# A four-layer graph network on one core: a leading dimension of 2 or 4 on the DRAM side of the loops' loads and stores

## The reference

```python
# layer 0: an MLP per edge, summed by destination
h = relu(concat(x[dst], x[src], edge_attr_32) @ W1 + b1)
out = segment_sum(h @ W2 + b2, dst)
# layer 1: degree-normalised sum over edges, by destination
agg = segment_sum(x[src] * ci[src][:, None], dst) * cj[:, None]
out = relu(where(in_deg > 0, agg, x) @ W.T + b)
# layer 2: symmetric normalisation, summed by source
agg = segment_sum(norm[:, None] * x[dst], src)
out = relu(agg @ W.T + b)
# layer 3: gates from the 40 edge features, a cutoff of the distance, summed by source
gate = silu(edge_attr_40 @ W1.T + b1) @ W2.T + b2 + adapt_logit
agg = segment_sum(gate * h[dst] * (cw * node_mult[dst])[:, None], src)
x = layernorm(x + layer(x))        # after each of the four
```

## Time and profile before

| | us |
|---|---|
| median of 3 runs | 24622.62 |
| lowest and highest | 24618.94, 24633.03 |
| span of the profiled execution, first to last instruction | 24578.9 |
| PE busy | 11303.0 (46%) |
| POOL busy | 11058.2 (45%) |
| DVE busy | 9805.1 (40%) |
| ACT busy | 3908.0 (16%) |
| DMA, queue row of SP (q1) | 9.9% of 16 engines |
| DMA, queue row of ScalarE (q10) | 4.6% of 16 engines |

### The profile page before, as it was taken

The page is one execution under the profiler, slowest core; times in us unless marked ns, Lnnn a source line. Parts: engine busy times, 40 slices in busy tenths (PEclk is TensorE's granted clock), DMA queues, the critical chain, the costliest instruction groups (busy, mean ns, idle before and its releaser), DMA issues. The chain is left out here.

```text
span 24578.9 us, 300511 instructions
## 1 busy us (share of the span) xinstructions
PE 11303.0 (46%) x63600; PEld 9551.4 (39%) x63601; DVE 9805.1 (40%) x26342; ACT 3908.0 (16%) x10412; POOL 11058.2 (45%) x11410
## 2 busy tenths in 40 slices
PE   5555555555544545555664333433532233333334
PEld 5555545454433333333443333333421133333334
DVE  3444444444555555551113444444411133333335
ACT  1000000000111111113331001100111122222221
POOL 3444444444433444435554444444344444444443
PEclk9999999999756566665555555555555555555555
DMA  4222222222111111113332111112222222121221
GB/s 97 66 64 66 65 66 65 65 65 65 43 31 32 34 34 35 34 32 92 89 89 60 54 53 55 54 54 55 58 64 57 58 57 56 54 56 56 55 57 47
DMA packets 1574947, 1407.00 MB, mean 57 GB/s; under 512 B 982793, under 2 KB 1441692, under 8 KB 1570447
## 3 DMA queue, kind: packets, MB, share of 16 engines
q1 hardware_dynamic: 597320, 636.63, 9.9%
q0 software_dynamic: 410000, 462.80, 7.9%
q10 hardware_dynamic: 567508, 306.27, 4.6%
HBM read 984.46 MB, written 420.15 MB: 57 GB/s over the span
## 5 line engine op out<-in xcount | busy, mean ns | idle before, releaser
L1743 POOL DMA_INDIRECT order<-l_msg,l_uring x6250 | 6046.0, 967 | 6894.5 <-ACT l_uring L2012 4152.7
L1886 PE MATMUL ps<-l_ordb,l_ohs 128*128 128x49 f32 x15040 | 3319.1, 413 | 4897.1 <-DVE acc L1786 3125.6
L1886 PEld LDWEIGHTS ps<-l_ordb,l_ohs 128*128 128x128 f32 x15040 | 3248.2, 331 | 4967.9 <-DVE acc L1786 3170.3
L545 POOL DMA_INDIRECT l_rows<-btab,l_sd x3125 | 2978.5, 953 | 3292.3 <-DMA l_sd<-in_sd 2081.4
L1786 DVE TENSOR_TENSOR acc<-acc,ps 128x49 f32 x7520 | 1526.5, 206 | 3901.5 <-DMA btab<-pro_stb 2159.2
L1082 POOL DMA_INDIRECT l_rows<-y,l_sd x1875 | 1828.2, 975 | 2733.2 <-DMA l_sd<-in_sd 2199.7
L701 PE MATMUL ps<-l_ohe,l_hid 128*128 128x32 f32 x6250 | 1372.3, 365 | 2538.9 <-issue 2537.6
L701 PEld LDWEIGHTS ps<-l_ohe,l_hid 128*128 128x128 f32 x6250 | 1436.5, 323 | 2492.0 <-issue 2491.7
L686 PE MATMUL ps<-l_rhs,l_lhs 64*128 x6250 | 1421.9, 423 | 280.2 <-issue 119.3
L1303 PE MATMUL ps<-l_okey,l_hlo 128*128 128x294 bf16 x2520 | 716.4, 405 | 1784.5 <-issue 647.7
L686 PEld LDWEIGHTS ps<-l_rhs,l_lhs 64*128 64x128 f32 x6250 | 1350.8, 328 | 341.7 <-issue 341.7
(11 more groups left out here) (313 smaller groups left out, 14418.7 us busy)
## 6 DMA issues: line engine op xcount, KB each, us to landing
l_ordb<-order SPq DMA_DIRECT2D x752, 250.0 KB
l_dstb<-ids SPq DMA_DIRECT2D x250, 600.0 KB
order<-l_msg,l_uring POOLq DMA_INDIRECT x6250
order<-l_zero ACTq DMA_DIRECT2D x125, 775.0 KB
l_eat<-in_ea40P SPq DMA_DIRECT2D x625, 120.0 KB
gates<-l_made ACTq DMA_DIRECT2D x625, 120.0 KB
l_gin<-gates SPq DMA_DIRECT2D x125, 600.0 KB
l_rows<-btab,l_sd POOLq DMA_INDIRECT x3125
```

The lines of the kernel that those rows point to most:

```text
L545: pool.indirect_dma_start(rows[:, t, :], None, d["btab"], bass.IndirectOffsetOnAxis(ap=sd[:, t, 0:1], axis=0)).then_inc(gat[c], 16)
L1743: pool.indirect_dma_start(d["order"], bass.IndirectOffsetOnAxis(ap=uring[:, t:t + 1], axis=0), msg[:, t, :], None).then_inc(sc[c], 16)
L1886: done = t.matmul(red[b % 2][:, k * MW:(k + 1) * MW], ohs[b][:, k, :], ordb[b][:, k, 0:MW], start=True, stop=True)
```

## The change

A helper `queues` gives the DRAM side of a transfer a leading dimension of 2 (`FEW`) or 4 (`SOME`): rows `(a p)` become `a` times `p`. It is put around 16 transfers that SP and ScalarE issue in the loops of the four layers; the SBUF side stays one dimension of partitions. Nothing else changes: same bytes, same buffers, same waits, same order.

```diff
--- before.py
+++ after.py
...
@@ -98,6 +98,16 @@
 
 def bc(ap, shape):
     return ap.to_broadcast(shape)
+
+
+FEW, SOME = 2, 4
+
+
+def queues(ap, k):
+
+    if len(ap.shape) == 2:
+        return ap.rearrange("(a p) f -> a p f", a=k)
+    return ap.rearrange("(a p) t f -> a p t f", a=k)
 
 
 def gnn(nc, a, out):
...
@@ -504,12 +514,12 @@
-                sp.dma_start(dstb[:, ds((g % 2) * GE, GE)], d["ids16"][0:1, ds(g * GE, GE)].to_broadcast([WN, GE])).then_inc(dstb_in, 16)
+                sp.dma_start(dstb[:, ds((g % 2) * GE, GE)], queues(d["ids16"][0:1, ds(g * GE, GE)].to_broadcast([WN, GE]), SOME)).then_inc(dstb_in, 16)
-                    sp.dma_start(sd[:, chunk_cols(c), :], a["sd"][:, ds(t0, CT), :]).then_inc(sd_in[c], 16)
+                    sp.dma_start(sd[:, chunk_cols(c), :].rearrange("p t k -> p (t k)"), queues(a["sd"][:, ds(t0, CT), :].rearrange("p t k -> p (t k)"), FEW)).then_inc(sd_in[c], 16)
...
@@ -519,7 +529,7 @@
-                                     d["atab"][ds(window_at(nc, pl, starts[c], k), WN), :]).then_inc(win_in, 16)
+                                     queues(d["atab"][ds(window_at(nc, pl, starts[c], k), WN), :], FEW)).then_inc(win_in, 16)
...
@@ -724,13 +734,13 @@
-                act.dma_start(lhs[WN:KW, :], a["ea32T"][:, ds(g * GE, GE)]).then_inc(eat_in, 16)
+                act.dma_start(lhs[WN:KW, :], queues(a["ea32T"][:, ds(g * GE, GE)], SOME)).then_inc(eat_in, 16)
-                    act.dma_start(d["esrc"][:, ds(g * GT + c * CT, CT), :], rows[:, chunk_cols(c), H0:BW]).then_inc(est[c], 16)
+                    act.dma_start(queues(d["esrc"][:, ds(g * GT + c * CT, CT), :], SOME), rows[:, chunk_cols(c), H0:BW]).then_inc(est[c], 16)
...
@@ -1032,12 +1042,12 @@
-                sp.dma_start(ids[:, ds(g % 2, 1), :, :].rearrange("p o t k -> p (o t) k"), a["sd"][:, ds(g * GT, GT), :]).then_inc(ids_in, 16)
+                sp.dma_start(ids[:, ds(g % 2, 1), :, :].rearrange("p o t k -> p (o t k)"), queues(a["sd"][:, ds(g * GT, GT), :].rearrange("p t k -> p (t k)"), FEW)).then_inc(ids_in, 16)
-                sp.dma_start(sd[:, ds(g % 2, 1), :, :].rearrange("p o t k -> p (o t) k"), a["sd"][:, ds(g * GT, ST), :]).then_inc(sd_in, 16)
+                sp.dma_start(sd[:, ds(g % 2, 1), :, :].rearrange("p o t k -> p (o t k)"), queues(a["sd"][:, ds(g * GT, ST), :].rearrange("p t k -> p (t k)"), FEW)).then_inc(sd_in, 16)
...
@@ -1057,7 +1067,7 @@
-                act.dma_start(order[:, ds(g * KZ, KZ)], zero[:, :]).then_inc(z_out, 16)
+                act.dma_start(queues(order[:, ds(g * KZ, KZ)], SOME), zero[:, :]).then_inc(z_out, 16)
...
@@ -1668,13 +1678,13 @@
-                    sp.dma_start(ordb[b][:, :, :], order[:, ds(n * RT + first[b], RB[b]), :]).then_inc(ord_in[b], 16)
+                    sp.dma_start(ordb[b][:, :, :].rearrange("p t f -> p (t f)"), queues(order[:, ds(n * RT + first[b], RB[b]), :].rearrange("p t f -> p (t f)"), SOME)).then_inc(ord_in[b], 16)
-                sp.dma_start(dstb[:, ds((g % 2) * GE, GE)], d["ids16"][0:1, ds(g * GE, GE)].to_broadcast([WK, GE])).then_inc(ids_in, 16)
+                sp.dma_start(dstb[:, ds((g % 2) * GE, GE)], queues(d["ids16"][0:1, ds(g * GE, GE)].to_broadcast([WK, GE]), SOME)).then_inc(ids_in, 16)
...
@@ -1684,10 +1694,10 @@
-                    sp.dma_start(dist[:, ds(g % 2, 1), :].rearrange("p o t -> p (o t)"), a["dist"][:, ds(g * GT, GT)]).then_inc(edge_in, 16)
-                    sp.dma_start(gin[:, ds(g % 2, 1), :, :].rearrange("p o t f -> p (o t f)"), d["gates"][:, ds(g * GT, GT), :].rearrange("p t f -> p (t f)")).then_inc(edge_in, 16)
+                    sp.dma_start(dist[:, ds(g % 2, 1), :].rearrange("p o t -> p (o t)"), queues(a["dist"][:, ds(g * GT, GT)], FEW)).then_inc(edge_in, 16)
+                    sp.dma_start(gin[:, ds(g % 2, 1), :, :].rearrange("p o t f -> p (o t f)"), queues(d["gates"][:, ds(g * GT, GT), :].rearrange("p t f -> p (t f)"), SOME)).then_inc(edge_in, 16)
-                    sp.dma_start(esr[:, ds(g % 2, 1), :, :].rearrange("p o t f -> p (o t f)"), d["esrc"][:, ds(g * GT, GT), :].rearrange("p t f -> p (t f)")).then_inc(edge_in, 16)
+                    sp.dma_start(esr[:, ds(g % 2, 1), :, :].rearrange("p o t f -> p (o t f)"), queues(d["esrc"][:, ds(g * GT, GT), :].rearrange("p t f -> p (t f)"), SOME)).then_inc(edge_in, 16)
...
@@ -1698,7 +1708,7 @@
-                        sp.dma_start(eat[:, j, c, :], a["ea40P"][:, ds(job(g, many, j) * (NCH * HE) + c * HE, HE)]).then_inc(ea_in[j][c], 16)
+                        sp.dma_start(eat[:, j, c, :], queues(a["ea40P"][:, ds(job(g, many, j) * (NCH * HE) + c * HE, HE)], SOME)).then_inc(ea_in[j][c], 16)
...
@@ -1979,7 +1989,7 @@
-                act.dma_start(d["gates"][:, ds(job(g, many, j) * GT + c * CT, CT), :].rearrange("p t f -> p (t f)"), made[:, h, :]).then_inc(made_out[h], 16)
+                act.dma_start(queues(d["gates"][:, ds(job(g, many, j) * GT + c * CT, CT), :].rearrange("p t f -> p (t f)"), SOME), made[:, h, :]).then_inc(made_out[h], 16)

```

## The result

| | before | after |
|---|---|---|
| median, us | 24627.82 (4 runs) | 24760.20 (4 runs) |
| lowest and highest | 24618.94, 24660.81 | 24736.87, 24785.92 |
| span of the profiled execution | 24578.9 | 24783.9 |

The ratio is 1.0053, interval 1.0041 to 1.0065: slower by 132 us (101 to 160). The forecast was 24910. The profiled execution of after is the slowest of its four (its own time is 24785.92, 2.0 us above its span), so the two profiles lie 205 us apart where the medians lie 132 apart.

The account below looks back on a forecast made before the run. The prediction took a chain of waits, walked once per group, to bound the kernel. 183 + 40 + 16 + 50 = 289 us on 24578.9, plus 43.7, gave 24911.6, predicted as 24910; its own range was 24780 to 25030.

Parts of the forecast that it names:

- Only `dstb` changes, 4 engines instead of 16.: Of the wrapped transfers only the 125 `dstb` loads of layer 0 and 250 of layers 2 and 3 change.
- A row takes 0.35 to 0.395 us, the load 9.0.: In layers 2 and 3, `dstb` puts 24 rows on each of 4 engines, taking 9.0 us.
- the rival's number: Quicker rows on four engines: 0.30 us a row, `dstb` 7.3 us, total 24783; chance 15%.
- The issue grows by 0.4 us.: Issuing `dstb` takes 0.4 us more than its 362 ns median; bounds 0 and 0.4.
- The windows land at 13.0.: The five window loads queue behind `dstb`, which ends at 10.4 us, and end 13.0 us behind its issue.
- Layer 2's first part, +4.7 a group, 183 us.: In layer 2's first 39 groups PE's look-up starts at 13.5 instead of 8.8 us: 4.7 later each, 183 us.
- Layer 3, two-block groups, +5.0 each, 40 us.: In 8 groups of layer 3's first part `gin` goes out about 5.0 us later, 40 us in all.
- The 31 others, 16 us.: Layer 3's 31 one-block groups, where windows are issued late, lose 0.5 us each, 16 us; bounds 0 and 2.0 each.
- Layer 0, 50 us.: In layer 0 `sd`, by which GpSimd starts, is held up 0.4 us in each of 125 groups, 50 us.
- Reading groups 0, layer 1 0.: SP's waits of 9.2 and 23.7 us in groups 40 to 124 swallow 5.6 us of lateness; layer 1 is unchanged.
- thin-cover rival: SP's cover in the 170 reading groups is too thin: 2 us lost each, 340 us more, 25250; chance 10%.
- The span lies 43.7 us below the median.: The median of the runs lies 43.7 us above the profiled span of 24578.9, so this was added to the forecast.

Follow-up runs that it names:

- e14_slow4: Kernel before with SP rereading the table entry ahead of each window load and `dstb` on 4 engines, in layers 2 and 3: 17553.12 us, ratio 1.0287.
- second pair of profiles: Kernel before (24832.59 us) and the same with `dstb` on 4 engines in layers 2 and 3 only (25041.83 us, ratio 1.0084), on one chip.
- e2_l0: Kernel before with `dstb` on 4 engines in layer 0 only: 17059.03 us, ratio 1.0000.
- full_again: The changed kernel as it is, run again beside the kernel before: 17388.79 us, ratio 1.0188.
- e5_two: Kernel before with `dstb` on 2 engines in layers 2 and 3 only: 25493.75 us, ratio 1.0266.

## Why the forecast was wrong in size

The direction and the place were right (slower, by `dstb`'s later landing in the first part of layer 2); the size was 288 us and is 132. Two steps failed. The larger is the cost of a row: 9.0 us for 24 rows, 0.375 each, carried over from 16 engines, where four engines take 0.27 to 0.30. The other is the path in layer 3's two-block groups, which were to pay 5.0 us each and paid nothing in the first pair of profiles (1.6 each in the second). And the wait that ends last was the wrong one: the windows by the forecast, the one-hots by the profile. By the steps of the prediction:

- **Only `dstb` changes, 4 engines instead of 16.** Right, by the 4,500 packets. (The diff wraps 15 transfers, not 16.)
- **A row takes 0.35 to 0.395 us, the load 9.0.** This is the step that failed first. With fewer engines a row is quicker: 0.27 to 0.30 us on 4, the rival's number, to which I gave 15%, and under the 0.3 that I had named as a sign of being wrong. The load takes 6.5 to 7.9 us, `dstb` ends 9.1 us behind its issue in layer 2's first part (medians) and not 10.4. The duration was read from one load by 16 engines that read the same DRAM row at once, and carried over to four. The rival's total, 24783, lies 23 us from the measured one, but not by its parts: it has 117 us in layer 2's first part, where 149 were measured, and 26 in the two-block groups, where nothing was.
- **The issue grows by 0.4 us.** Right: +0.42 (782 ns against 362).
- **The windows land at 13.0.** They land at 10.8. Besides the quicker rows the 2.6 us for the five windows behind `dstb` were too many: the last one lands 1.7 us behind `dstb`. That they come behind it is right: in layer 3's reading groups the first window packet starts at 8.1 us and `dstb` ends at 8.1 (medians). That SP's own issues are held up was not in the forecast.
- **Layer 2's first part, +4.7 a group, 183 us.** Measured 3.8, 149 us, and 122 on another chip. The one-hots (551 us of PE's idle time), not the windows (31), are what PE waits for; I had put the windows last. In the quick condition it is 4.5.
- **Layer 3, two-block groups, +5.0 each, 40 us.** Measured -1 us by the profiles (+13 on the other chip). I said that the queue decides since the last window is issued by 6.5 us. But with the load done 7.1 us behind the issue instead of 10.4 (median of the 8), the last window is hardly behind anything: it lands at 8.6, where it was 7.6. By the records `dstb`'s packets start 0.2 us behind the issue there and not 1.5; in the profile of before they even start 1.1 us ahead of it, so the record of a slow issue comes late and the two can't be set off to the microsecond. On the other chip, where `dstb` is done at 9.1, the windows land 3.0 us later. e14_slow4 shows what covers the load in the quick condition: a slow SP between `dstb` and the last window swallows the price.
- **The 31 others, 16 us.** Measured 15, and 5 in the second pair of profiles: 0.5 us a group is less than what these pairs can tell.
- **Layer 0, 50 us.** Measured -22 in the shown pair and 0 in the quick condition, where GpSimd hardly waits for SP. In the slow condition GpSimd's start moved to 2.98 us behind `sd`'s issue from 2.47 (one group each, at 2951.52 and at 3011.39), as forecast, but the group as a whole isn't longer: GpSimd idled 3119 us in the stage before and 3091 after. What ate the 0.4 us there no run tells; a difference under some 30 us isn't told from what layer 1 varied by.
- **Reading groups 0, layer 1 0.** Somewhat too low for the reading groups: +13 and +24 by the first pair of profiles, +35 and +25 by the second, where layer 1, which did not change, moved by +27 and -13; I had said within 10. In the quick condition, where it can be told, they cost +10 each. (The lateness of 5.6 us counts the dearer issue twice, since the 13.0 us of the windows have it already.) The thin-cover rival, 2 us a group and 340 in all, falls: even 2 engines cost 80 there.
- **The span lies 43.7 us below the median.** A wrong reading. Every run with both figures has its time some 2 us above its span; the rest of the 43.7 is by how much the profiled execution was quicker than the median.

The sum closes in this way. By the two profiles the forecast was 289 us and the change 205, 84 too many: 34 in layer 2's first part, 42 in layer 3's, 72 in layer 0, less 64 in layer 1 and the reading stages, which moved up without a forecast. The other 67 us of the 151 between 24911.6 and 24760.2 are no mechanism: the profiled execution of after lies 24 us above its median, measured by its span, and that of before 44 below.

What stays open is layer 0's -22 us, and why in the slow condition the medians of one pair show 132 us for the whole change and those of another 204 for layers 2 and 3 alone, where the profiles of both pairs show 200 for these layers; no third pair was run there.

## What to carry to other kernels

Before pricing a longer transfer, look at what its consumer waits for last, and at how long the issuer takes to send what stands between the two: the same four-engine load costs 3.9 us a group with a quick issuer (307 us in 78 groups), 0.7 with one that takes 5 us longer between them (56 us), and at most 0.3 when it is issued a group ahead (22 us for the whole program). A wait in every group's head is better taken away by issuing it a group earlier (here 2.0% in the quick condition, for another order of a few lines), down to what the next engine allows: here GpSimd's 31.0 us a group. And don't scale the time of a row on 16 engines to 4 without a row of a load that has four.

## What the runs showed of the hardware

- The same program took 17.06 ms on three chips and 24.6 to 24.8 ms in two other sets of runs, with nearly equal busy times (PE 11204 us in e2_l0, 11303 in the profile of before) and granted clocks (0.656 and 0.652); one of nine executions on a chip that otherwise gave 17.06 took 23.9. In the slow condition 992 of SP's 5,392 register moves, 123 of its 901 branches and 607 of its 4,497 semaphore instructions take 0.6 to 0.8 us (medians 0.03, 0.05 and 0.02); in e2_l0 none does. A profile should be looked at for such steps before a plan is built on it.
- Rows of 6,400 bytes from one place in DRAM, in layers 2 and 3: 0.35 to 0.40 us each with 16 engines at work, 0.29 to 0.31 with 8, 0.27 to 0.30 with 4, 0.26 to 0.27 with 2, which is 16 to 18, 21 to 22, 21 to 24 and 24 GB/s for one engine. The quickest row takes 0.241 us (26.6 GB/s) in before, in after and in e5_two alike. The Trainium skill ("DMA: Bandwidth & Descriptors", "Specifications") gives about 27 GiB/s for an engine, 29 GB/s; none of these rows reached it.
- The issue of `dstb` with the additional dimension on its DRAM side costs 0.69 to 0.84 us against 0.33 to 0.36 without it (medians of the stages in which SP isn't slow), with 16, 8, 4 and 2 engines.
- While the long rows are under way, SP's window issues take longer: five took 6.95 us and not 4.80, one up to 3003 ns. In layer 2's first part the five of a group take 4.0 us in all in e2_l0 (16 engines), 7.1 in full_again (4) and 11.8 in e5_two (2), and the last of them ends 0.4 us behind the long rows in the latter two (medians). The issuer is held up too, not only the transfer.
